# State sums of a selective scan: two states at once in TensorE's 64x64 tiling, joined by a permutation; other slots, carry on ScalarE

## The reference

```python
x = silu(conv4(in_proj_x(norm(h))))          # z = in_proj_z(norm(h))
dt_r, B, C = split(x_proj(x))                # 16, 16, 16 per head
delta = softplus(dt_proj(dt_r) + dt_b)
s = s * exp(delta * A) + (delta * x) * B     # 16 states per channel, along the tokens
y = sum_n(s[n] * C[n])                       # the sum over states
out = ((y + x * Dskip) * silu(z)) @ out_proj.T
```

## Time and profile before

| | |
|---|---|
| median of 3 runs | 5081.26 us (5041.83 to 5086.45) |
| the profiled execution's own time | 5077.92 us |
| its span | 5076.1 us |
| busy: PE, DVE, POOL, ACT | 88%, 92%, 80%, 67% |
| TensorE clock granted, mean | 0.974 |

### The profile page before, as it was taken

How to read it: one execution, slowest core, us unless ns; L and a number is a source line. 1 busy time by engine, 2 the same in 40 slices (tenths; PEclk the granted TensorE clock), 3 DMA queues, 4 the chain that set the end, 5 groups by cost and what they waited for, 6 DMA issues and landing times.

```text
span 5076.1 us, 53787 instructions
## 1 busy us (share of the span) xinstructions
PE 4473.4 (88%) x13617; PEld 2317.4 (46%) x13868; DVE 4671.7 (92%) x6890; ACT 3397.6 (67%) x5527; POOL 4073.1 (80%) x2833
## 2 busy tenths in 40 slices
PE   4789989989988998998899899899988989988987
PEld 1334444444444444444444444444444444444444
DVE  6999999999999999999999999999999999999995
ACT  4766666667676666766766666676666667676664
POOL 5888888888888887888888888788788888888884
PEclk9999999999999999999999999999999999999999
DMA  2333333333333333333333333333333333333330
GB/s 92 142 124 118 121 119 118 122 122 121 119 121 123 119 124 120 122 118 123 121 118 120 124 118 122 118 122 119 118 123 117 122 121 122 119 122 121 118 122 32
DMA packets 211097, 599.91 MB, mean 118 GB/s; under 512 B 25446, under 2 KB 76774, under 8 KB 210790
## 3 DMA queue, kind: packets, MB, share of 16 engines
q1 hardware_dynamic: 209088, 594.30, 33.8%
q10 hardware_dynamic: 1702, 2.16, 0.2%
HBM read 575.39 MB, written 20.97 MB: 117 GB/s over the span
## 4 chain that ended last, share of the span: by engine, by line
PE 45%; DVE 25%; ACT 14%; issue 11%; POOL 4%; DMA 0%; DVEq 0%; ACTq 0%; another core or an unknown queue 0%; POOLq 0%
DVE state L827 14%; PE ybank L894 13%; PE pbank L918 9%; ACT decay L422 5%; PE bank_c L904 5%; DVE db L817 4%; PE bank_a L1009 4%; PE db L882 3%; PE pbank L904 3%; PE bank_b L962 3%; POOL prod L604 2%; PE bank_a L995 2%; DVE carry L832 2%; ACT L546 1%; ACT L541 1%
## 5 line engine op out<-in xcount | busy, mean ns | idle before, releaser
L604 POOL TENSOR_TENSOR prod<-state,cs 128x1024 f32<-128x1024 f32 x1024 | 2415.7, 2359 | 832.0 <-DVE state L827 823.3
L422 ACT ACTIVATE decay<-delta,aneg 128x512 f32<-128x512 f32 x2048 | 1415.9, 715 | 692.8 <-DVE state L827 689.2
L817 DVE TENSOR_TENSOR db<-db,du 128x512 f32<-128x512 f32 x2048 | 1399.7, 683 | 198.7 <-remote 130.0
L894 PE MATMUL ybank<-prod,ident 128*128 128x512 f32 x3072 | 1567.6, 621 | 5.9 <-POOL prod L604 2.2
L827 DVE TENSOR_TENSOR_SCAN state<-decay,carry,db 128x512 f32<-128x512 f32 x1024 | 1288.2, 1258 | 0.0
L827 DVE TENSOR_TENSOR_SCAN state<-decay,db 128x512 f32<-128x512 f32 x1024 | 1230.0, 1201 | 0.0
L882 PE MATMUL db<-pieces,sel 128*128 128x512 bf16 x1799 | 691.2, 385 | 477.3 <-DVE state L827 471.4
L894 PEld LDWEIGHTS ybank<-prod,ident 128*128 128x128 f32 x3072 | 604.6, 198 | 350.7 <-issue 282.0
L608 POOL TENSOR_TENSOR prod<-prod 128x512 f32<-128x512 f32 x512 | 651.5, 1272 | 40.1
L882 PEld LDWEIGHTS db<-pieces,sel 128*128 128x128 bf16 x2048 | 199.2, 97 | 863.7 <-DVE state L827 692.1
L1009 PE MATMUL bank_a<-wd,ht 128*128 128x256 f32 x1536 | 413.6, 380 | 1.2 <-ACT ht L472 1.2
(11 more groups left out here) (118 smaller groups left out, 6007.8 us busy)
## 6 DMA issues: line engine op xcount, KB each, us to landing
cs<-c_rows SPq DMA_DIRECT2D x1024, 512.0 KB, 3.6
xin<-in_hidden SPq DMA_DIRECT2D x128, 128.0 KB, 2.4
xres<-in_hidden SPq DMA_DIRECT2D x128, 128.0 KB, 3.3
out_x<-ot SPq DMA_DIRECT2D x128, 128.0 KB, 2.4
c_rows<-xdbl SPq DMA_DIRECT2D x128, 32.0 KB, 3.6
win<-in_win_t SPq DMA_DIRECT2D x1, 1024.0 KB, 10.1
state<-in_w_gate ACTq DMA_DIRECT2D x1, 704.0 KB
state<-in_w_up ACTq DMA_DIRECT2D x1, 704.0 KB
```

Source lines behind the costliest of these rows:

```text
L422: act.activation(decay[:, g.val() % RING, :], delta[:, gu % 2, :], ACT.Exp, scale=aneg[:, gu % HEADS, gn:gn + 1]).then_inc(decayed, 1)
L604: pool.tensor_tensor(prod[:, r, :, :], state[:, 2 * p:2 * p + 2, :], cs[:, c, :, :], ALU.mult).then_inc(weighted, 1)
L817: dve.tensor_tensor(t[:, :], t[:, :], du[:, gu % 2, :], ALU.mult).then_inc(db_done, 1)
L894: last = pe.matmul(ybank[:, :], ident[:, :], prod[:, p % P_RING, k, :], start=(p == 0), stop=(p == PAIRS - 1 and k == 1))
```

## The change

- `sum_up` uses four tiles of 64x64 of the array for a pair. State k of the pair and half r of the partitions: state 0 goes straight (half r to half r of `ybank`), state 1 crosswise (half r to half 1-r of `cross`, the former `bank_c`). The sums of the eight pairs are issued in four groups of two pairs at slots 8, 12, 16 and 19. GpSimd's additions are gone.
- ScalarE copies `cross` into SBUF at slot 20 (`ycross`, which lies in the buffer `xlate`), and TensorE adds it, with the halves changed back by the matrix `swap`, into `ybank` at slot 21. VectorE takes the result at slot 22, GpSimd's product follows at 23.
- The carry is copied by ScalarE in two halves of eight states, at slots 9 and 17; VectorE waits for a half before it overwrites these states.
- In-projection z goes to `bank_a`, the magnitudes of the first quantisation to `bank_b`, those of the hidden vector to `cross`.
- Slots: second up product 40 to 37, its product with silu 41 to 38, magnitudes 48/50 to 53/54, rounding 49/51 to 54/55, GpSimd's last scaling 53 to 57, down product 73-76 to 70-72, output addition 77 to 73, the last convolution tap 10 to 11.

```diff
-ADDED = (0, 2, 4, 6)
+SUMS = {8: (0, 1), 12: (2, 3), 16: (4, 5), 19: (6, 7)}
+Q = P // 2
...
+def carry_count(u, half):
+    return 2 * (u.val() // PER * HEADS + u.mod(HEADS)) + half + 1
...
+                for half, slot in ((0, 9), (1, 17)):
+                    if w := due("scan", slot):
+                        if early_chunk(w):
+                            rows = slice(half * HALF_ST, (half + 1) * HALF_ST)
+                            wait(act, scanned, w.val(NST, (half + 1) * HALF_ST))
+                            act.activation(carry[:, w.mod(HEADS), rows], state[:, rows, CH - 1],
+                                           ACT.Copy).then_inc(carried, 1)
...
+                if w := due("scan", 20):
+                    wait(act, summed, w.val(PAIRS, PAIRS))
+                    wait(act, joined, w.val())
+                    wait(act, conv_mm, min(w.val(plus=3), UNITS))
+                    act.activation(ycross, cross[:, :], ACT.Copy).then_inc(cross_taken, 1)
...
-                if p in ADDED:
-                    wait(pool, weighted, w.val(PAIRS, p + 1))
-                    pool.tensor_tensor(prod[:, r, 0, :], prod[:, r, 0, :], prod[:, r, 1, :],
-                                       ALU.add).then_inc(added, 1)
...
-                if w := due("scan", 19):
-                    wait(dve, summed, w.val(PAIRS, PAIRS))
+                if w := due("scan", 22):
+                    wait(dve, joined, w.val(plus=1))
...
-                for part, slot in ((0, 49), (1, 51)):
+                for part, slot in ((0, 54), (1, 55)):
...
+                    if n % HALF_ST == 0 and (u + -1).within(UNITS) and early_chunk(u + -1):
+                        wait(dve, carried, carry_count(u + -1, n // HALF_ST))
...
-                if n == NST - 1 and g.within(STEPS) and not late:
-                    wait(dve, scanned, g.val(plus=1))
-                    dve.tensor_copy(carry[:, h, :], state[:, :, CH - 1]).then_inc(carried, 1)
-                    wait(dve, carried, u.div(PER, HEADS, h + 1))
...
+                for slot, pairs in SUMS.items():
+                    if w := due("scan", slot):
+                        sum_up(w, pairs)
...
-            def sum_up(w, p):
...
-                for k in range(1 if p in ADDED else 2):
-                    last = pe.matmul(ybank[:, :], ident[:, :], prod[:, p % P_RING, k, :],
-                                     start=(p == 0), stop=(p == PAIRS - 1 and k == 1))
-                last.then_inc(summed, 1)
+            def sum_up(w, pairs):
+                for p in pairs:
+                    if p == 0:
+                        wait(pe, y_taken, w.val())
+                        wait(pe, cross_taken, w.val())
+                        wait(pe, h_round, min((w + -7).val(4, 4), 4 * TILES))
                     wait(pe, weighted, w.val(PAIRS, p + 1))
+                    for k in range(2):
+                        for r in range(2):
+                            rows = slice(r * Q, (r + 1) * Q)
+                            c = r ^ k
+                            last = pe.matmul((ybank, cross)[k][c * Q:(c + 1) * Q, :], ident[rows, rows],
+                                             prod[rows, p % P_RING, k, :], start=(p == 0), stop=(k == 1 and p == PAIRS - 1),
+                                             tile_position=(r * Q, c * Q), skip_group_check=True)
+                    last.then_inc(summed, 1)
...
                 if v := due("pre", 10):
-                    wait(pe, sz_done, v.val())
-                    wait(pe, v_round, (v + -7).val(2, 2))
+                    wait(pe, o_done, v.val(plus=-9))
...
+                if w := due("scan", 21):
+                    wait(pe, cross_taken, w.val(plus=1))
+                    pe.matmul(ybank[:, :], swap[:, :], ycross, start=False, stop=True,
+                              skip_group_check=True).then_inc(joined, 1)
...
-                for slot, ks in ((73, (0,)), (74, (1,)), (75, (2, 3)), (76, (4, 5))):
+                for slot, ks in ((70, (0, 1)), (71, (2, 3)), (72, (4, 5))):
...
                         if heads[0] == 0:
                             wait(pe, yg_done, t.div(4, 4, 4))
-                            wait(pe, o_done, t.val(plus=-3))
+                            if (t + 6).within(UNITS):
+                                wait(pe, sz_done, t.val(plus=7))
```

More of the change, by code:

```diff
@@ L196, in build @@
         pbank = bank("pbank")
-        bank_c = bank("bank_c")
+        cross = bank("cross")
         bank_a = bank("bank_a")
@@ L476, in step @@
                     wait(act, v_norm, t.val(plus=1))
[L477 to L481, removed]
-                    wait(act, h_norm, t.val(plus=1))
[L483 to L490, removed]
+                    wait(act, h_op, t.val(2))
+                    act.activation(bank_b[:, 0:DM], v2[:, :], ACT.Abs, scale=POWER).then_inc(v_abs, 1)
+                if t := due("post", 53):
+                    wait(act, h_norm, t.val(plus=1))
+                    wait(act, h_round, t.val(4))
+                    wait(act, cross_taken, min(t.val(plus=7), UNITS))
+                    act.activation(cross[:, 0:HALF], hv[t.mod(2)][:, 0:HALF], ACT.Abs, scale=POWER).then_inc(h_abs, 1)
+                if t := due("post", 54):
                     wait(act, h_round, t.val(4, 2))
-                    act.activation(bank_c[:, 0:HALF], hv[t.mod(2)][:, HALF:INNER], ACT.Abs, scale=POWER).then_inc(h_abs, 1)
+                    act.activation(cross[:, 0:HALF], hv[t.mod(2)][:, HALF:INNER], ACT.Abs, scale=POWER).then_inc(h_abs, 1)
                 if t := due("post", 28):
@@ L503, in step @@
                     wait(act, conv_mm, v.val())
+                    wait(act, joined, v.val(plus=-2))
                     if v.mod(PER) < HEADS:
@@ L796, in behind @@
                     block_scale(hs).then_inc(h_scale, 1)
-                for part, slot in ((0, 49), (1, 51)):
+                for part, slot in ((0, 54), (1, 55)):
                     if t := due("post", slot):
                         wait(dve, h_round, t.val(4, 2 * part + 1))
-                        step_down(HALF, hv[t.mod(2)][:, part * HALF:(part + 1) * HALF]).then_inc(h_round, 1)
+                        step_down(cross, HALF, hv[t.mod(2)][:, part * HALF:(part + 1) * HALF]).then_inc(h_round, 1)
             def step(b, j, n):
@@ L903, in in_proj @@
                     h = v.mod(HEADS)
-                    return pe.matmul((pbank, bank_c)[part][:, :], win[:, k, part * DI + h * P:part * DI + (h + 1) * P],
+                    return pe.matmul((pbank, bank_a)[part][:, :], win[:, k, part * DI + h * P:part * DI + (h + 1) * P],
                                      xnt[:, v.mod(8) // 4, k, :], start=(k == 0), stop=(k == KM - 1))
@@ L912, in side @@
                     in_proj(v, 0, 1).then_inc(x_mm, 1)
-                for slot, taps in ((9, (0, 1)), (10, (2, 3))):
+                for slot, taps in ((9, (0, 1)), (10, (2,)), (11, (3,))):
                     if v := due("pre", slot):
@@ L952, in side @@
                     last.then_inc(xn_tp, 1)
-                for part, slot in ((0, 35), (1, 40)):
+                for part, slot in ((0, 35), (1, 37)):
                     if t := due("post", slot):
```

65 lines of the change are left out of this document (34 added, 31 removed).

## The result

The changed kernel takes 4895.01 us (median of 4 runs, 4890.4 to 4896.46) against 5076.49: a ratio of 0.9653 with a 95% interval of 0.9606 to 0.97, 181 us less. The forecast was 4852.

What follows compares the result with a forecast made beforehand. VectorE (92% busy) and TensorE (88%) were taken to bound the kernel in turn. The sum was 5077.9 - 98 (carry) - 128 (waits) = 4852 us; own range 4730 to 4960, wider range 4730 to 5220.

Steps and rivals of the forecast that it cites:

- The tiles overlap: TensorE's state sums: a pair's four 64x64 tiles run at once, 0.86 us a pair, 2.04 a group with drains.
- The first rival: TensorE's sums: the two halves of each fp32 matmul follow each other, 3.87 us a group, 5470 us in all; chance 0.18.
- the second: TensorE's sums: tiles do not overlap at all, 27.5 us of sums a unit, about 6900 us in all; chance 0.04.
- the eight weight loads: TensorE, each pair of sums: loads at an estimated 0.1 us each, 0.8 us, fit just under the pair's 0.86.
- The waits for spreads and for the state sum go: VectorE's waits for TensorE: 1.3 us a unit for spreads and 0.34 for the state sum vanish.
- The new wait for the up product: Slot 3: the group of sums ahead delays the up product to 3.6 us, VectorE wants it at 2.3; 1.2 us a unit.
- The second magnitude: ScalarE, second rounding: magnitude ends about 12.3 us, VectorE asks at 12.0; a wait of 0.25 us.
- The carry, 98 us: VectorE's carry copy goes to ScalarE: 1.53 us saved in each of 64 early units, 98 us.
- GpSimd's additions are worth nothing themselves: GpSimd: removing 5.1 us of additions a unit gains nothing itself, as they are off the path.
- 98 + 128 = 226 us: Forecast savings: 98 us from VectorE's carry copy, 128 us from VectorE waiting 1.0 us a unit less over 128 units.
- The third rival: VectorE: groups cost 2.6 to 3.0 us, waits reach 3 us a unit, only the carry pays: 5010 us; chance 0.14.

## Why the prediction was right, step by step

**The tiles overlap: right.** A group cost 1.97 us for a forecast 2.04, and the order of issue does not matter. The first rival (halves in series, 3.87 a group) and the second (no overlap) were wrong about the engine. One term was right for a reason that did not hold: the eight weight loads were to fit under a pair in a row, at an estimated 0.1 us each. They take 0.134 us and would not fit, but they run side by side, four at a time. The rule of program order that spoke for the first rival was read in the Trainium skill, TensorE: Matmul & The Clock Gate, Part 3; for records of different tiles page and measurement differ, and the measurement decides: the second halves of the first tile do not hold the first halves of the others, in either order of issue.

**The waits for spreads and for the state sum go: right in the main.** From 1.3 us a unit to 22.6 / 108.6 = 0.2, and from 0.34 to nothing. The prediction put this down to the spread of TensorE's load over the slots, and that is borne out: with the additions back in the new slots, the load of sums as before, 0.5 us a unit of spread waits is left. With two full matmuls a pair it is 1.9 us.

**The new wait for the up product: right in place and cause, somewhat short.** 160.6 / 108.6 = 1.48 us a unit for a forecast 1.2. The four float32 records behind the group last 1.45 us together where 1.35 is usual, and I had let the data be there with the distance of starts, not with the end of the last record. The prediction's own terms also gave 3.6 - 2.3 = 1.3, not 1.2. In all VectorE idles 197.8 / 108.6 = 1.82 us a unit, 1.45 had been forecast: 0.37 x 128 = 47 us, about the 43 between forecast and result; its work, 3802.18 / 108.6 = 35.0 us a unit, came as forecast (35.8 less half of 1.53).

**The second magnitude: right in place, half as large.** It is 0.22 us where it occurs, 0.25 were forecast; but it occurs in every second unit (52 times in 108.6 units), so that the mean of the stage is 0.1.

**The carry, 98 us: right as VectorE's work, wrong as the price of the carry.** In the kernel before it was worth 126 us, about half by the copy itself (0.94 us each and not 1.53, as VectorE makes up part of it) and about half by the clock, which fell behind most copies; the row with four records of 2.81 us was in the trace and I had not looked for what follows a copy. In the changed kernel it is worth 19 to 27, as the copy would have shrunk to 366 ns there. As the price of the carry 98 us was off in both kernels; as a piece of VectorE's work it held. I had taken the copy's length for its own. The row of the tile said 359 ns at the least beside a median of 1370, and I quoted it without asking what made the difference. And "GpSimd's additions are worth nothing themselves" was wrong: they were on the path through the copy.

**The attribution.** I summed 98 + 128 = 226 us, and 181 were measured. The experiments give 126 for the carry and 60 for all the rest taken after it (4955.61 to 4895.01), which is itself the tiling's 178 less the 118 that join, cross copy and new slots cost without it. So the right mechanisms stand beside shares that were not right, 98 for 126 and 128 for 60. The total came out near because it is an account of VectorE's work and waits in the changed kernel, and these came nearly as forecast (35.0 us of work, 1.82 of waits for 1.45). What each part is worth by itself depends on what the others leave, and to that the prediction had no answer.

**The third rival** (new waits eat the gain) was half true: of the gain on spreads and sum, 1.3 - 0.2 + 0.34 = 1.4 us a unit, the gated product's wait took 0.85 back (1.48 now for 65.6 / 104.5 = 0.63 before).

Its price was mis-summed as well: 3 us of waits a unit where there were 2.44 give 5078 - 98 + 72 = 5052 us, not 5010, and the chances for faster add up to 0.64 + 0.06 = 0.70, not 0.68. Neither touches the 4852.

**What was behind the new wait** was not in the prediction: taking it away alone brought 7 us (18 by the ratio). ScalarE was late by nearly as much right behind it. Both together brought 128 us.

## What to carry to other kernels

Before an instruction's mean is used as a price, look at its least value: where the two are far apart, the difference belongs to a neighbour, and changing the operation's kind (here a reduction for a copy, one line, 121 us) may be worth as much as moving it. Where two engines are late at nearly the same time, mending the later one gives little; read what would end the wait next, and the next wait too. Where matmuls only add, four 64x64 tiles do two 128-row sums in the time of one, plus a fixed 0.25 to 0.28 us for each change into the tiling and back, and here a copy and one joining matmul a unit. Put the groups behind whatever the bound engine waits for next.

## What the runs showed of the hardware

- Four 64x64 tiles of float32 run at once with both record halves: starts within 0.02 to 0.04 us, 0.43 us a step, in both orders of the stream that were tried. A group between full matmuls costs 0.25 to 0.28 us on top. The weight loads of the four tiles (134 ns each) run side by side as well.
- Taking 16 strided values on VectorE lasted 178 to 182 ns as a reduction, with GpSimd working beside it in all 64 cases. As a copy it lasted 175 ns with GpSimd idle; begun while an operation of GpSimd ran, it ended some 30 ns behind that one in all 124 cases of two kernels, after 357 to 1389 ns.
- After 2.40 us of waiting TensorE ran a stretch at the lower clock level: 2.81 us for four records instead of 1.88. In the kernel before, 40 of 53 falls of the clock came within 8 us behind a carry copy; without the long copy there were 18.
